# A transformer layer on 8 cores: cast-on-load FFN weights, and two elementwise operations moved from GpSimd to VectorE

## The reference

```python
y   = _layernorm(x)                            # x: 16 x 2048 x 1024
h   = _layernorm(y) * norm_w + norm_b
qkv = h @ qkv_w.T + qkv_b                      # qkv_w: 3072 x 1024
q, k, v = qkv.reshape(B, L, 3, D)              # one head
w = softmax(einsum('ncq,nck->nqk', q, k / sqrt(2048)), axis=2)   # 1024 x 1024 for a sequence
a = einsum('nqk,nck->ncq', w, v)
x   = x + (a @ proj_w.T + proj_b + y)
z   = _layernorm(x)
h   = float2fix(z @ w1 + b1)                   # w1: 1024 x 4096
h   = pwlin_gelu(h)                            # piecewise-linear GELU, on multiples of 2^-8
out = float2fix(h @ w2 + b2)                   # w2: 4096 x 1024
x   = x + out
```

## Time and profile before

| | |
|---|---|
| median of 3 runs | 3716.23 us |
| the profiled execution | 3714.03 us |
| its span on the slowest core (core 5) | 3712.5 us |
| spans of the eight cores | 3690.8 to 3712.5 us |
| TensorE matmul busy | 2127.0 us, 57% |
| VectorE busy | 1347.8 us, 36% |
| ScalarE busy | 1120.3 us, 30% |
| GpSimd busy | 117.3 us, 3% |
| start, up to the first L349 matmul | 0 to 354 us |
| last projection tile to first FFN matmul | 1764 to 1836 us |

### The profile page before, as it was taken

How to read it: one execution, slowest core, us unless ns; L and a number is a source line. 1 busy time by engine, 2 the same in 40 slices (tenths; PEclk the granted TensorE clock), 3 DMA queues, 4 the chain that set the end, 5 groups by cost and what they waited for, 6 DMA issues and landing times.

```text
span 3712.5 us, 27628 instructions; the slowest of 8 cores (3690.8 to 3712.5 us)
## 1 busy us (share of the span) xinstructions
PE 2127.0 (57%) x8086; PEld 819.8 (22%) x8086; DVE 1347.8 (36%) x2436; ACT 1120.3 (30%) x1865; POOL 117.3 (3%) x170
## 2 busy tenths in 40 slices
PE   2001029776764966766175665656756566565664
PEld 2000003232321322322021222212222122221221
DVE  0000643220142322014164462644626546265362
ACT  0000210001130000113174471744717447175371
POOL 0000000001110000111100000000000000000000
PEclk9999559887886988888587887878878788786886
DMA  9998570100056010014601002010020100201101
GB/s 108 108 108 107 156 138 1 23 0 1 23 170 125 1 23 1 0 37 170 212 1 51 29 9 72 1 51 29 4 77 1 51 29 3 77 1 51 34 1 63
DMA packets 193568, 199.08 MB, mean 54 GB/s; under 512 B 156422, under 2 KB 156550, under 8 KB 191370
## 3 DMA queue, kind: packets, MB, share of 16 engines
q1 hardware_dynamic: 170540, 105.03, 12.4%
q0 software_dynamic: 4448, 50.33, 9.7%
q10 hardware_dynamic: 18432, 41.95, 3.1%
HBM read 151.14 MB, written 75.50 MB: 61 GB/s over the span
## 4 chain that ended last, share of the span: by engine, by line
PE 38%; ACT 16%; DVE 15%; DMA 9%; issue 8%; SPq 7%; another core or an unknown queue 4%; POOL 2%; ACTq 1%; DVEq 1%; POOLq 0%
PE pf L808 8%; PE pf L932 6%; PE pf L489 6%; SPq L266 6%; DMA ys<-fX 4%; ACT yt L883 4%; PE pf L632 4%; PE pf L524 3%; PE pf L573 3%; ACT hs0f L855 2%; ACT hs1f L855 2%; PE pf L896 2%; DVE hs0f L863 1%; DVE hs0f L866 1%
## 5 line engine op out<-in xcount | busy, mean ns | idle before, releaser
L808 PE MATMUL pf<-z2cm,w1b 128*128 128x512 bf16 x2048 | 613.6, 455 | 517.7 <-ACT hs0f L821 269.0
L808 PEld LDWEIGHTS pf<-z2cm,w1b 128*128 128x128 bf16 x2048 | 207.0, 109 | 899.9 <-issue 764.9
L896 PE MATMUL pf<-w2b,yt 128*128 128x512 bf16 x1024 | 339.1, 465 | 112.5 <-ACT yt L883 112.5
L932 PE MATMUL pf<-w2b,yt 128*128 128x512 bf16 x1024 | 249.7, 405 | 113.8 <-DVE fY1I L957 113.8
L489 PE MATMUL pf<-W1q,xcm 128*128 128x512 bf16 x1024 | 236.5, 385 | 48.2 <-DVE xcm L470 48.2
L821 ACT ACTIVATE hs0f<-pf,st_b1adj 128x512 f32<-128x512 f32 x128 | 85.7, 670 | 536.5 <-DVE fX L962 475.0
L957 DVE CAST fY1I<-pf 128x512 int32<-128x512 f32 x64 | 44.3, 692 | 449.0 <-PE pf L941 268.8
L590 ACT ACT_TABLE_LOAD x2 | 2.6, 1283 | 627.6 <-DVE mbc L582 627.6
L896 PEld LDWEIGHTS pf<-w2b,yt 128*128 128x128 bf16 x1024 | 117.7, 117 | 315.5 <-issue 252.5
L671 PE MATMUL pf<-pwT,acm 128*128 128x512 bf16 x512 | 142.6, 429 | 66.9 <-DVE x1t L697 64.2
L932 PEld LDWEIGHTS pf<-w2b,yt 128*128 128x128 bf16 x1024 | 104.7, 102 | 261.6 <-issue 155.6
(11 more groups left out here) (126 smaller groups left out, 2713.2 us busy)
## 6 DMA issues: line engine op xcount, KB each, us to landing
xst<-xs SPq DMA_DIRECT2D x64, 512.0 KB, 3.7
x1b<-x1scr SPq DMA_DIRECT2D x64, 512.0 KB, 3.8
x1scr<-x1t ACTq DMA_DIRECT2D x32, 512.0 KB, 4.9
ys<-fX ACTq DMA_DIRECT2D x64, 256.0 KB, 3.5
x16scr<-xs POOLq DMA_DIRECT2D x2, 4096.0 KB, 63.3
w116scr<-w POOLq DMA_DIRECT2D x1, 8192.0 KB, 237.4
w216scr<-w POOLq DMA_DIRECT2D x1, 8192.0 KB, 312.4
z2scr<-z2t ACTq DMA_DIRECT2D x32, 256.0 KB, 2.5
```

The source lines that it names most:

```text
L808: t.matmul(pf[:, off:off + 512], w1b[:, j, 128 * ft:128 * (ft + 1)], z2cm[:, j, :], start=(j == 0), stop=(j == ND - 1)))
L896: t.matmul(pf[:, off2:off2 + 512], yt[:, ftw, 128 * tt:128 * (tt + 1)], w2b[:, ftw, 0:512], start=(ftw == 0), stop=False))
L932: t.matmul(pf[:, off:off + 512], yt[:, ft, 128 * tt:128 * (tt + 1)], w2b[:, ft, 512:1024], start=(ft == 0), stop=False))
```

## The change

The bf16 copies of w1 and w2 in DRAM are gone. The loads of `w1b` and `w2b` read the f32 inputs directly and cast on the way into SBUF; they stay at the same place in GpSimd's list. The two scaling operations L607 (`Wn`) and L741 (`z2t`) go from GpSimd to VectorE, with their semaphores; the rest of GpSimd's small operations stays.

```diff
-        inc("gpsimd", "dCWS", 16, lambda g: g.dma_start(out=w116scr, in_=w1))
-        v_wcast = inc("gpsimd", "dCWS", 16, lambda g: g.dma_start(out=w216scr, in_=w2))
...
-                wait_drain("gpsimd", ("Wn",))
-                wait("gpsimd", "cDV", v_rcc)
+                wait_drain("vector", ("Wn",))
                 dvn = 0
                 for hh in range(2):
-                    dvn = inc("gpsimd", "cPL", 1,
-                              lambda g_, p=p, hh=hh:
-                              g_.tensor_scalar(out=Wn[:, 512 * hh:512 * (hh + 1)],
+                    dvn = inc("vector", "cDV", 1,
+                              lambda v_, p=p, hh=hh:
+                              v_.tensor_scalar(out=Wn[:, 512 * hh:512 * (hh + 1)],
                                                in0=pth16[:, 512 * hh:512 * (hh + 1)],
                                                scalar1=rcc[p][:], scalar2=None, op0=ALU.mult))
-                add_drain(("pth",), "cPL", dvn)
-                wait("tensor", "cPL", dvn)
+                add_drain(("pth",), "cDV", dvn)
+                wait("tensor", "cDV", dvn)
...
-                wait_drain("gpsimd", ("z2t", zbuf))
-                wait("gpsimd", "cDV", v_s2)
-                dvz = inc("gpsimd", "cPL", 1,
-                          lambda g_, g=g, x1buf=x1buf, zbuf=zbuf:
-                          g_.tensor_scalar(out=z2t[zbuf][:], in0=x1t[x1buf][:],
+                wait_drain("vector", ("z2t", zbuf))
+                dvz = inc("vector", "cDV", 1,
+                          lambda v_, g=g, x1buf=x1buf, zbuf=zbuf:
+                          v_.tensor_scalar(out=z2t[zbuf][:], in0=x1t[x1buf][:],
                                            scalar1=ST["m2n"][:, g:g + 1], scalar2=ST["s2"][:, g:g + 1],
                                            op0=ALU.add, op1=ALU.mult))
-                drain[("x1t", x1buf)] = [("cPL", dvz), (f"dX1S{x1buf}", v_x1st[b]), ("cAC", vsq)]
-                wait("scalar", "cPL", dvz)
+                drain[("x1t", x1buf)] = [("cDV", dvz), (f"dX1S{x1buf}", v_x1st[b]), ("cAC", vsq)]
+                wait("scalar", "cDV", dvz)
...
-        wait("gpsimd", "dCWS", v_wcast)
         v_w1b = 0
         for j in range(ND):
             v_w1b = inc("gpsimd", "dCW", 16,
-                        lambda g, j=j: g.dma_start(out=w1b[:, j, :], in_=w116scr[128 * j:128 * (j + 1), :]))
+                        lambda g, j=j: g.dma_start(out=w1b[:, j, :], in_=w1[128 * j:128 * (j + 1), :]))
         wait("gpsimd", "cPE", v_projpe[1])
         v_w2b = 0
         for jj in range(8):
             v_w2b = inc("gpsimd", "dCW2", 16,
                         lambda g, jj=jj: g.dma_start(
                             out=w2b[:, 4 * jj:4 * (jj + 1), :],
-                            in_=w216scr[512 * jj:512 * (jj + 1), :].rearrange("(c p) n -> p c n", p=128)))
+                            in_=w2[512 * jj:512 * (jj + 1), :].rearrange("(c p) n -> p c n", p=128)))
```

More of the change, by code:

```diff
@@ L97, in build_program @@
     pw16scr = nc.dram_tensor("pw16scr", [D, D], BF16, kind="Internal").ap()
-    w116scr = nc.dram_tensor("w116scr", [D, FF], BF16, kind="Internal").ap()
-    w216scr = nc.dram_tensor("w216scr", [FF, D], BF16, kind="Internal").ap()
     x1scr = nc.dram_tensor("x1scr", [T, D], F32, kind="Internal").ap()
@@ L191, in build_program @@
                      "dTB0", "dTB1", "dTZ", "dCX0", "dCX1", "dCQ", "dCP",
-                     "dCW", "dCW2", "dCWS", "dZ20", "dZ21", "dX1S0", "dX1S1",
+                     "dCW", "dCW2", "dZ20", "dZ21", "dX1S0", "dX1S1",
                      "dX1L", "dOUT", "cPE", "cDV", "cAC", "cPL"]
```

## The result

The changed kernel takes 3575.74 us, the median of ten runs, against 3714.48 us for the kernel before (ten runs). The ratio is 0.9598 with a 95% interval of 0.9576 to 0.9621: 4.0% faster. By the ratio the kernel stands at 0.9598 x 3714.48 = 3565 us. The forecast was 3626 us, its own range 3605 to 3650, and the range with the rivals 3565 to 3670: the measured time lies at the lower edge of this wider one.

A forecast was written before the change was run, and what follows sets the result against it. No engine was the bound; waits were, chiefly cast traffic at the start and the load before the FFN. 3714.0 - 153.4 + 100.7 - 41 + 10 - 4 - 2.2 = 3624.1, forecast 3626 us, own range 3605 to 3650, with rivals 3565 to 3670.

The forecast's parts named there:

- rival A: Load of w1b and w2b: only bytes read count, so it takes 109 us, kernel 3578 us; chance 0.26.
- GpSimd's shorter list: Before the FFN: GpSimd's last operation ends sooner, so the loads start 2.2 us earlier.
- Part 1: Kernel start: without the casts of w1 and w2 the queue drains sooner and everything after moves as a block, -153.4 us.
- rival D: Kernel start doesn't shorten, the 170.8 us being the transposes' own time; 3779 us, chance 0.02.
- Part 2: Load before the FFN: casting at 109 GB/s written takes 157 us in place of 56.3, all exposed, +100.7 us.
- Rival B: Load before the FFN: the cast gets slower in small pieces, +31 to +46 us, 3657 to 3672 us; chance 0.10.
- rival C: Load before the FFN takes over 247 us, under 68 GB/s written, making the kernel slower than before; chance 0.04.
- Part 3: Attention tiles: reciprocal to transposes takes 1.13 us in place of 3.69, saving 41 us over 16 tiles.
- clock term: Attention: TensorE's low-clock stretch keeps its 10.2 us, so more matmuls run at half speed, +10 us (0 to +21).
- Rival E: Attention: the shorter idle gap no longer makes TensorE's clock fall, saving 36 us; 3580 us, chance 0.04.
- Part 4: Projection tiles: the scaled residual falls from 1.53 to 0.81 us without GpSimd's `z2t`; -0.13 us a tile, -4 us for 32.

The follow-up runs named there:

- added copies: Changed kernel plus one unawaited DMA per attention stage, copying w1 within DRAM: plain f32 in the first, casting in the second; 95.8 and 72.2 us on core 0.

## Why the prediction was right, and where its number was off

The direction held. The range held at its lower edge, and not by the forecast's mechanism: what came true in the largest uncertain term is rival A, to which I had given 0.26 against 0.54, and the measured time lies 40 us under the forecast's own range. The range reached down to it because it was drawn to hold A. The number was 61 us too high by the ratio, 72 us on core 5, and one term carries most of that.

| term | forecast | measured, core 5 |
|---|---|---|
| casts leave the start | -153.4 | -153.7 |
| casting load | +100.7 | +49.5 |
| `Wn` on VectorE | -41 | -39.7 (2.48 x 16) |
| clock in attention | +10 | +4.0 (0.25 x 16) |
| `z2t` on VectorE | -4 | -6.7 (0.21 x 32) |
| GpSimd's shorter list | -2.2 | -2.1 |
| everything else | 0 | -13.4 |
| sum | -89.9 | -162.1 |

*Part 1, the start*, was right to 0.3 us, and rival D is out. What stands behind the last cast moved as a block: the first transpose was still held until the proj_w copy was through, at 161 us, now for 19.47 us.

*Part 2, the load*, is the step that failed. I took 109 GB/s written from the casts at the start since "the operation is the same, only the destination differs". The destination was the point. The start's 109 GB/s is a limit on what passes to and from DRAM, 218 read and 109 written; with SBUF as the target the written half doesn't count, and the load read 328 GB/s. The added copies show it apart from the change: 350 GB/s plain, 349 GB/s with a cast, on core 0. This is rival A, and its 109 us for the load against 105.8 measured would have given 3578 us. I had its evidence, 327 and 317 GB/s in two very different stages, and called it an accident of the mix. What A said in words, that only bytes read count, holds for a target in SBUF alone. The Trainium skill ("DMA: Bandwidth & Descriptors", Specifications) gives a limit of about 358 GB/s of HBM traffic for one core. The runs here lie on both sides of that figure: 328 GB/s in the loads, 327 in the casts at the start, and 337 to 378 in the added copies. So a limit on DRAM traffic was the right thing to reckon with, and its size is shown here only to within some 10%. What sets it, the pair of cores at one memory or something in a core's own path, these runs don't separate, since the cores did the same at nearly the same time.

*Rival B* (small pieces cost) and *rival C* are out: the load's 1 MB pieces from rows of 4 KB were cast at 164 GB/s written, the 8 MB copies at 109.

*Part 3, `Wn`*: 1.21 us against 1.13 forecast, the pair 0.61 against 0.62. The clock term had the right sign and 40% of its size. That the low stretch keeps its 10.2 us came true in nine of sixteen tiles; in the other seven it was 6.8 us, and what decides between the two no run shows. Rival E is out: with a gap of 4.83 us the clock still falls in every tile of core 5, and the second product never takes less than 8.35 us there.

*Part 4, `z2t`*: both operations at 0.81 us as forecast; the waits between them overlap more than I had taken, 0.21 us a tile in place of 0.13.

*The rest*, 13.4 us, has no term. 11.7 of it is the FFN stage, which no edit touches. On core 5 it was long before (1876.1; the other seven cores had 1865.8 to 1872.2). Some 6 us of it go with `Wn`: the median of the eight cores is 1869.3, 1870.0 and 1869.5 us in the kernels with `Wn` on GpSimd (before, the weights alone, `z2t` alone), and 1863.2 and 1864.4 in those with it on VectorE (`Wn` alone, the changed kernel run again). No run explains these 6 us; it stays open.

## What to carry to other kernels

Before pricing a DMA that was moved, ask which of its two ends counts: here bytes to and from DRAM shared about 330 to 350 GB/s, so the casts of w1 and w2 in DRAM cost 154 us, the same casts into SBUF 106, and no cost of the cast itself showed. A transfer is dear or free by where it is issued: the copies that held up the start for 154 us cost nothing beside an attention stage without DMAs, where they took 152, and that beat leaving them out by 48 us. An operation moved from an idle engine to a busier one can leave that one no later, where the two had slowed each other: VectorE's scaled residual took 1.53 us beside GpSimd's `z2t` and 0.81 without it.

## What the runs showed of the hardware that was not expected

- An f32 copy within DRAM is slower than a copy with a cast to bf16 (95.8 against 72.2 us for 16.78 MB read, on core 0; the same order on all eight).
- TensorE's clock in attention doesn't settle into an alternation: L627 goes 9.71, 9.88, 9.98, 8.35 us, with low stretches of 10.2 or 6.8 us; before it alternated between 8.7 and 9.9. In the second attention cores 4 and 5 run through the same eight times to 0.01 us, from 8.75 up to 10.0 and back to 8.37.
- Bulk loads from GpSimd's queue hold back small loads from SyncE's: 15.5 us in place of 3.6 for 512 KB, and at the start a transpose of some 3 us stood for 19.5 us until the last cast was through.
